# Two semaphores and a wait ahead of each indirect scatter in the routing of the expert layers

## What is computed

```
logits = norm(x) @ Wg + bg                       # [4096 tokens, 8]
top2   = the two largest of each token's logits; share = softmax over these two
y      = sum over the two experts e of share[e] * expert_e(norm(x))
layer 1: expert_e = relu(x @ W1[e] + b1[e]) @ W2[e] + b2[e]
layer 3: expert_e = (silu(gate) * up) @ w2[e],   gate, up = halves of x @ w1[e]
```

## Time and profile before

| | |
|---|---|
| timed, median of 3 (lowest, highest) | 3513.22 us (3511.18, 3513.64) |
| profiled execution, first to last instruction | 3632.7 us |
| PE busy in the profile | 3010.8 us, 83% (24093 instructions) |
| DVE, ACT, POOL busy | 2320.2, 1697.5 and 1319.8 us |
| DMA queue of POOL (q0) | 12432 packets, 34.10 MB |
| DMA queue of SP (q1) | 183648 packets, 266.40 MB |

### The profile page before, as it was taken

The page is one execution under the profiler, slowest core; times in us unless marked ns, Lnnn a source line. Parts: engine busy times, 40 slices in busy tenths (PEclk is TensorE's granted clock), DMA queues, the critical chain, the costliest instruction groups (busy, mean ns, idle before and its releaser), DMA issues. The chain is left out here.

```text
span 3632.7 us, 74176 instructions
## 1 busy us (share of the span) xinstructions
PE 3010.8 (83%) x24093; PEld 2134.9 (59%) x24102; DVE 2320.2 (64%) x5140; ACT 1697.5 (47%) x2908; POOL 1319.8 (36%) x1326
## 2 busy tenths in 40 slices
PE   6996899999979998399978999995564899835983
PEld 5885232232238887289966777773343677624883
DVE  6887566666335664014438888877997899832564
ACT  4774788888834442033323444442444566510110
POOL 1111455556514440520003333320435677533023
PEclk9998999999989997599989999997787899967997
DMA  2001444444333203332231111110000433112334
GB/s 102 16 14 34 118 133 121 124 125 130 99 142 117 100 18 126 126 138 72 70 123 51 56 51 53 50 40 16 1 0 19 175 117 117 65 41 94 98 103 133
DMA packets 196205, 302.07 MB, mean 83 GB/s; under 512 B 24560, under 2 KB 133232, under 8 KB 189808
## 3 DMA queue, kind: packets, MB, share of 16 engines
q1 hardware_dynamic: 183648, 266.40, 23.4%
q0 software_dynamic: 12432, 34.10, 2.9%
HBM read 216.51 MB, written 75.50 MB: 80 GB/s over the span
## 5 line engine op out<-in xcount | busy, mean ns | idle before, releaser
L2518 ACT ACTIVATE params<-L0f_Z,params 128x1024 f32<-128x1024 f32 x512 | 532.6, 1113 | 83.9 <-PE L0f_Z L2574 83.7
L2495 POOL TENSOR_TENSOR L0f_mixed<-L0f_mixed,L0f_gated 128x512 f32<-128x512 f32 x240 | 332.1, 1384 | 291.6 <-DVE L0f_gated L2738 291.3
L2574 PE MATMUL L0f_Z<-params,L0f_w_stacked 128*128 128x512 f16 x1024 | 296.9, 388 | 34.1 <-ACT params L2518 23.2
L2738 DVE SCALAR_TENSOR_TENSOR L0f_gated<-L0f_O,params 128x512 f32<-128x512 f32 x240 | 180.0, 750 | 224.0 <-PE L0f_O L2583 147.9
L2583 PE MATMUL L0f_O<-params 128*32 128x512 f32 x2048 | 275.1, 609 | 0.4 <-ACT params L2518 0.4
L860 POOL TENSOR_TENSOR params<-params,L2x_recip_den 128x512 f32<-128x512 f32 x128 | 134.8, 1053 | 353.8 <-DVE L2x_recip_den L1115 353.3
L2574 PEld LDWEIGHTS L0f_Z<-params,L0f_w_stacked 128*128 128x128 f16 x1024 | 70.6, 98 | 289.6 <-ACT params L2518 265.9
L2209 PE MATMUL L3ftiles_H<-L3ftiles_rowsT,L3ftiles_w_tile 128*128 128x128 f32 x1296 | 166.9, 284 | 51.0 <-DVE L3ftiles_rowsT L2237 36.0
L2209 PEld LDWEIGHTS L3ftiles_H<-L3ftiles_rowsT,L3ftiles_w_tile 128*128 128x128 f32 x1296 | 161.8, 199 | 63.1 <-DVE L3ftiles_rowsT L2237 41.1
L2880 POOL TENSOR_SCALAR L2f_hidden_int<-params 128x1024 bf16<-128x1024 f32 x32 | 119.2, 3724 | 200.1 <-ACT params L2907 198.2
L1848 PE MATMUL L1fprepare_K<-L1fprepare_ctxT,params 128*128 128x256 f32 x512 | 130.1, 414 | 59.4 <-issue 51.4
(11 more groups left out here) (508 smaller groups left out, 7698.5 us busy)
## 6 DMA issues: line engine op xcount, KB each, us to landing
params<-gates_dram SPq DMA_DIRECT2D x512, 128.0 KB, 3.2
params<-side_dram SPq DMA_DIRECT2D x32, 1024.0 KB, 4.8
keysT_dram<-L1fprepare_keysT SPq DMA_DIRECT2D x32, 512.0 KB
params<-keysT_dram SPq DMA_DIRECT2D x32, 512.0 KB
rows_in_dram<-L1x_zero SPq DMA_DIRECT2D x30, 512.0 KB, 3.3
L3ftiles_rows<-rows_in_dram SPq DMA_DIRECT2D x84, 128.0 KB
rows_out_dram<-L3ftiles_outputs SPq DMA_DIRECT2D x80, 128.0 KB
L1ftiles_rows<-rows_in_dram SPq DMA_DIRECT2D x76, 128.0 KB
```

The source lines that it names most:

```text
L2495: pool.tensor_tensor(acc[:, b.slot, m % KT, :], acc[:, b.slot, m % KT, :], tmp[:, m % 2, :], ALU.add).then_inc(mixed, 1)
L2518: act.activation(hid[:, n % 4, :, :], Z[:, n % 2, :, :], ACT.Gelu, bias=w["b1"][:, n // 4:n // 4 + 1]).then_inc(hid_ready, 1)
L2574: mm = pe.matmul(Z[:, n % 2, s, :], w1s[:, e, :], stack[:, b.slot, t, 2 * half + s, :], start=True, stop=True)
L2738: dve.scalar_tensor_tensor(out=out, in0=O[:, m % 2, :], scalar=w["b2"][:, e:e + 1], in1=gb[:, e % AHEAD, m % KT, :], op0=ALU.add, op1=ALU. ...
```

## The change

The loop over batch rows and slots becomes one loop over n = 0 to 2 HALF - 1. Scatters of slot 0 raise one semaphore, those of slot 1 another. Ahead of each scatter, from the third on, POOL waits until all earlier scatters of the same slot have landed; so scatter n is issued only when scatter n - 2 has landed, and at most two are in flight. After the loop POOL waits for both semaphores. As `prepare` serves both phases, the change holds for the 64 scatters of layer 1 and for the first 32 of layer 3. The other 32 of layer 3, and all gathers, are not changed.

```diff
--- before.py
+++ after.py
@@ -1724,7 +1724,7 @@
             "xn_ready", "xn_turned", "xnT_ready", "logits_ready", "logits_out", "norm_step"))
         step, exped, centered, chosen_ready, counted = (core.sem(s) for s in (
             "place_step", "logits_exped", "logits_centered", "chosen_ready", "tokens_counted"))
-        placed, scattered = core.sem("slots_ready"), core.sem("rows_scattered")
+        placed, scattered = core.sem("slots_ready"), [core.sem(f"rows{k}_scattered") for k in range(2)]
         if keys_ahead:
             KG, KTILES = 2, 4
             T = KG * P
@@ -1779,11 +1779,14 @@
         def _(pool):
 
             pool.wait_ge(placed, 1)
-            for b in range(HALF):
-                for k in range(2):
-                    pool.indirect_dma_start(out=rows_in[0], out_offset=bass.IndirectOffsetOnAxis(ap=slot[:, k, b:b + 1], axis=0),
-                                            in_=kept[:, b, :], in_offset=None).then_inc(scattered, 16)
-            pool.wait_ge(scattered, 2 * HALF * 16)
+            for n in range(2 * HALF):
+                b, k = n // 2, n % 2
+                if b:
+                    pool.wait_ge(scattered[k], b * 16)
+                pool.indirect_dma_start(out=rows_in[0], out_offset=bass.IndirectOffsetOnAxis(ap=slot[:, k, b:b + 1], axis=0),
+                                        in_=kept[:, b, :], in_offset=None).then_inc(scattered[k], 16)
+            for k in range(2):
+                pool.wait_ge(scattered[k], HALF * 16)
 
         @block.scalar
         def _(act):
```

## The result

The changed kernel takes 3541.5 us (median of 4 runs, 3539.8 to 3547.0) against 3512.25 us for the kernel before (4 runs beside it): ratio 1.0088, 95% interval 1.0076 to 1.0101, so +29.3 us. The forecast was +19.7 us, 3533 us: the sign and the round trip as what costs were right and the total lay in the forecast's own range.

What follows compares the result with a forecast made beforehand. It took layer 1's block, timed, to end with the paced scatters and layer 3's burst to be paid in full; 11.5 + 8.2 = +19.7 us on 3513.2 us gave 3533 us, range 3460 to 3630 us.

Steps and rivals of the forecast that it cites:

- the forecast's own range: Whole kernel: 3520 to 3580 us for R around 3.2 to 4.2 us without a timed stall; chance 0.40.
- R: Both bursts: a scatter's time from issue to landing plus POOL's restart behind a wait; taken as 3.22 us.
- the real stall: Rival, layer 1's burst: stall also in timed runs, pacing ends it; -47.3 us, 3466 us at R = 3.22; chance 0.30.
- passing at once: Rival, both bursts: the waits pass nearly at once, no change; 3515.5 us with R = 2.85; chance 0.16.
- the long landing of 5.23 us: Rival, both bursts: landing takes what the burst's tail showed, R = 5.23, no stall; 3629 us; chance 0.14.
- Layer 1: Layer 1's block: timed, it ends with the scatters at 1547.7 instead of the keys at 1536.2, 11.5 us longer.
- The block's end: Behind the last scatters: waits cost nothing beyond the last landing, and a block change costs 1.03 us.
- The cover: Layer 1 before the change, without the stall: keys land at 1536.2, after the scatters at 1528.2.
- Layer 3's term: Layer 3's burst, with no work to cover it: scatters land at 3285.6 instead of 3277.43, 8.2 us longer.
- the short bound of 2.85 us: Layer 3's last scatter: data moved by 3274.5 plus 0.55 us to land, so 2.58 us, R = 2.85.
- The gap of 119.5 us: Whole kernel: profile longer than timed runs, 100.1 us of it laid to stalls mostly absent when nothing is recorded.
- a stall in layer 3's tiles: Layer 3's tiles beside the unchanged second burst: 33.1 us more in the profile, expected to stay after the change.

Runs made afterwards that it cites:

- the earlier trace: First profiled execution of the unchanged kernel before: span 3632.7 us, against a median of 3513.22 us in three timed runs.
- the two undisturbed traces: The kernel before, unchanged and profiled once more (timed 3510.7 us, span 3508.0 us), and the changed kernel (3541.5 us, span 3539.9 us).
- the other two undisturbed traces: Against the kernel before: two semaphores without waits between scatters, 3511.7 us; waits between scatters in layer 3's routing alone, 3513.15 us.

## Why the forecast came out as it did

**The mechanism** is as forecast in the burst: scatter k+2 starts one round trip R after scatter k; layer 3 pays in full; two semaphores are free. It is not as forecast at the end of layer 1's block. There the keys were to end the block before the change, 8.0 us after the scatters' landing (1536.2 - 1528.2), and to cover that much; undisturbed, keys and GpSimd end nearly together. The rivals fall: the real stall, because it isn't there; passing at once, because R is above 2.53 us even alone; the long landing of 5.23 us, because those 4.96 us were 2.5 us of landing and 3.5 us of GpSimd's block end, less the 1.03 us that I had taken off for a block change. The trace of the kernel before had that already, behind the last scatter of the earlier trace rows:

```profile
L1709 POOLq DRAIN  x1: 2665/2665/2665, 3275.1 to 3275.1; - x1
```

GpSimd has passed its wait for the last landing by 3275.1, 2.6 us after the scatter's start, and spends the next 2.67 us in the DRAIN.

**Layer 1** was to cost 11.5 us and, from the two undisturbed traces, costs 118.68 - 90.75 = 27.9 us from its first scatter to the next block. Three terms were off, all to the same side:
- R. At 3.22 us the last scatter starts 101.8 us after the first; it started 109.97 us after it, 8.2 us more. Paced but without other traffic it would have been 84.24 us: so 25.7 of the 29.6 us by which the burst grew come from the keys' traffic and only 3.9 us from two in flight as such. My rows could not show it: the stretch in which I looked for the load on the DMA engines was the disturbed one, with 122 GB/s in place of 286.
- The block's end. I took landing and block change at 4.0 us (3.22 - 0.27 + 1.03); it is 8.7 us: 4.7 us more.
- The cover. I put the next block 94.3 us after the first scatter (1536.2 + 1.03 - 1442.94); undisturbed it is 90.75 us, 3.5 us less. There GpSimd's DRAIN is over at 1530.5 (1525.2 + 5.28), only 1.1 us before SyncE has seen the last keys landed (1531.6). In the other two undisturbed traces GpSimd is the later one by 0.1 to 0.2 us, and against their 89.10 and 89.26 us the change costs layer 1 29.5 us, the whole growth of the burst. So the keys cover 1.7 us of it at most.

8.2 + 4.7 + 3.5 = 16.4, and 11.5 + 16.4 = 27.9 us. Layer 3's term errs the other way by 6 us, so the total is closer than its parts, and that is luck.

**Layer 3** was to cost 8.2 us and cost 47.79 - 45.64 = 2.15 us in the trace. There R is 2.67 us, not 3.22: the gather that I had chosen as the nearest row was no guide, and the short bound of 2.85 us was. R alone takes off 7.9 us (41.71 in place of 49.6). The block's end, 6.08 us where the sum had 4.2, gives back 1.9 us.

**One R for both layers** is thus the first step that failed (3.22 us, where layer 3 has 2.67 us and layer 1 beside the keys 3.80 us); the block's end without GpSimd's DRAIN is the second, and the cover of 8.0 us by the keys, where there is 1.7 us at most, the third. The Trainium skill (DMA: Bandwidth & Descriptors, Anatomy of one DMA) had 2.30 us to landing by estimate. Where the engines are otherwise idle the trace comes close, where they aren't it doesn't; layer 3 (3190 to 3230) and layer 1 (1445 to 1530) in the changed kernel, the last number being the median to landing in us:

```profile
rows_in_dram<-L3f_normalized,L3f_slots POOLq DMA_INDIRECT x31, 2.4
```

```profile
rows_in_dram<-L1f_normalized,L1f_slots POOLq DMA_INDIRECT x46, 2.9
```

**The gap of 119.5 us** I read rightly as time that isn't in the timed runs, and so held the stall out of the sum; that decided the sign. The sign was right for a wrong reason, and so in part by luck. The reason that I gave, that recording PE's instructions makes its signals late, is refuted: it made me expect a span near 3585 us (it was 3539.9) and a stall in layer 3's tiles (there is none). The Trainium skill (Runtime: NRT & Kernel Launch, The ~15µs preamble/postamble breakdown) has a profile's total some 6.2 us longer than the reported time, whatever the kernel. The span used here, from first to last instruction, is another measure, 1.9 us shorter than the timed run, so these runs don't test the page's figure; the 119.5 us are no such constant. What made TensorE's signals 8 us late in that one execution stays open.

## What to carry to other kernels

A wait on the last but one DMA costs what the round trip exceeds two issues by, and that round trip is not one number: read it in each stage, under that stage's own traffic, and by its spread rather than its mean (four in flight cost nothing that could be told here, three 9.6 us, two 29.3 us, one 157.1 us). Before resting on a profiled execution whose span is far from the timed runs, profile it again; the sizes in the stretch that looks ill are no guide to the others. And ask of a tail behind a burst which part is landing and which the engine's end of its block: one small instruction behind the last wait tells, and so do the DRAIN rows at the block's own line.

## What was not expected of the hardware

- A scatter of 131 KB lands 2.4 us after its issue whether one or two are in flight; where stores of 512 KB and loads of 256 KB bring the traffic to about 260 GB/s, scatters included, it takes from that to over 5 us.
- The next block begins 3.4 us after GpSimd's last instruction behind 32 scatters and 6.0 to 6.1 us behind 64. 2.8 and 5.4 us of that are its DRAIN. Why that takes longer with more scatters was not tried out.
- Waits that are already met add nothing to the 0.30 us that lies between two scatters anyway.
